# Eight attention rounds in another order on four engines, one Trainium2 core

## The reference

```python
x = L0(x)   # B=8, C=64, 16x16 pixels: N=256
            # q,k = Wq x + bq, Wk x + bk (8 channels); v = Wv x + bv (32 channels)
            # attn = softmax(q^T k); out = Wo (v attn^T) + bo; x = gamma*out + x
x = L1(x)   # the same with v of 64 channels and no Wo; x = x + out
x = L2(x)   # batch norm, relu, 3x3 conv with w = mean|w0| * sign(w0); again with w1; + x
x = L3(x)   # whitening by a Cholesky factor over 4 groups of channels, a 4x4 mix, bias
```

## Time and profile before

| | |
|---|---|
| median of 3 runs | 75.25 us (75.05 to 75.28) |
| profiled execution | 74.86 us, span 73.1 us |
| PE, PEld | 61.4 us (84%), 34.8 us (48%) |
| DVE, ACT, POOL | 50.4 us (69%), 46.6 us (64%), 26.9 us (37%) |
| mean of one DVE instruction | L877 684 ns, L901 684 ns, L887 482 ns, L907 422 ns, L917 484 ns |
| ACT, L458 | 446 ns, with 204 ns of reading the sum beside the next |
| fillers (L583) | six from 0.76 us on took 2.72 us, twelve from 42.90 us on 3.00 us |

### The profile page before, as it was taken

The page is one execution under the profiler, slowest core; times in us unless marked ns, Lnnn a source line. Parts: engine busy times, 40 slices in busy tenths (PEclk is TensorE's granted clock), DMA queues, the critical chain, the costliest instruction groups (busy, mean ns, idle before and its releaser), DMA issues.

```text
span 73.1 us, 1583 instructions
## 1 busy us (share of the span) xinstructions
PE 61.4 (84%) x512; PEld 34.8 (48%) x516; DVE 50.4 (69%) x134; ACT 46.6 (64%) x135; POOL 26.9 (37%) x68
## 2 busy tenths in 40 slices
PE   5968677489998999896939999799999889999910
PEld 2224534154553646444415573586745676774400
DVE  0067998587979888776993656899578994367340
ACT  1603589679898989899987527950069493535440
POOL 7005128702748475723050624460054600006300
PEclk9999999999999999999999999999999999999996
DMA  0888820000000000000000000000000000000025
GB/s 6 244 255 234 306 96 0 0 0 0 0 0 9 4 0 0 0 9 0 0 0 9 0 0 0 0 0 9 0 0 0 0 0 0 9 0 0 0 83 204
DMA packets 2167, 2.70 MB, mean 37 GB/s; under 512 B 368, under 2 KB 1520, under 8 KB 2160
## 3 DMA queue, kind: packets, MB, share of 16 engines
q1 hardware_dynamic: 1872, 2.41, 10.2%
q10 hardware_dynamic: 288, 0.20, 0.8%
HBM read 2.08 MB, written 0.52 MB: 36 GB/s over the span
## 4 chain that ended last, share of the span: by engine, by line
PE 49%; DVE 16%; ACT 13%; POOL 8%; issue 8%; POOLq 0%; ACTq 0%; DVEq 0%
PE bank L583 9%; PE bank L683 8%; ACT bank L458 7%; PE bank L739 5%; PE bank L593 4%; PE bank L617 4%; DVE cut L887 3%; PE bank L664 3%; PE bank L728 3%; DVE conv_in L991 3%; DVE conv_in L997 3%; ACT conv_in L511 2%; PE bank L764 2%; PE bank L772 2%; PE bank L649 2%
## 5 line engine op out<-in xcount | busy, mean ns | idle before, releaser
L458 ACT ACTIVATE bank<-bank,negmax 128x256 f32<-128x256 f32 x32 | 14.3, 446 | 1.2 <-DVE negmax L877 1.0
L583 PE MATMUL bank<-const-bfloat16-1.0 128*128 128x512 bf16 x52 | 14.1, 409 | 1.0 <-PEq L1164 0.8
L877 DVE TENSOR_REDUCE negmax<-bank 128x2 f32<-128x512 f32 x16 | 10.4, 684 | 1.4 <-PE bank L633 1.3
L739 PE MATMUL bank<-conv_in,taps 128*64 128x256 f16 x144 | 9.8, 279 | 1.0 <-DVE conv_in L997 0.7
L583 PEld LDWEIGHTS bank<-const-bfloat16-1.0 128*128 128x128 bf16 x56 | 5.6, 107 | 7.2 <-issue 2.5
L471 ACT ACTIVATE probs<-bank 128x512 f32<-128x512 f32 x16 | 8.6, 588 | 0.6 <-PE bank L654 0.5
L739 PEld LDWEIGHTS bank<-conv_in,taps 128*64 128x64 bf16 x144 | 7.3, 109 | 3.4 <-DVE conv_in L997 2.0
L683 PE MATMUL bank<-probs,vt 128*64 128x256 f32 x64 | 8.7, 391 | 0.0
L887 DVE TENSOR_SCALAR cut<-bank,prm 128x256 f32<-128x256 f32 x8 | 3.9, 482 | 5.8 <-PE bank L593 5.7
L511 ACT ACTIVATE conv_in<-z,bn_t,rstd 64x256 f16<-64x256 f32 x4 | 2.4, 601 | 6.8 <-POOL rstd L400 6.7
L458 ACT ACTIVATION_READ_ACCUMULATOR bank<-bank,negmax 128x1 f32 x32 | 6.5, 204 | 0.0
(11 more groups left out here) (130 smaller groups left out, 105.9 us busy)
## 6 DMA issues: line engine op xcount, KB each, us to landing
cw<-conv_w SPq DMA_DIRECT2D x2, 288.0 KB, 4.6
x<-x_in SPq DMA_DIRECT2D x4, 128.0 KB, 2.9
out<-res SPq DMA_DIRECT2D x2, 256.0 KB, 2.1
kst<-consts SPq DMA_DIRECT2D x1, 452.0 KB, 5.5
aw<-attn_w ACTq DMA_DIRECT2D x1, 128.0 KB, 2.5
aw<-attn_w SPq DMA_DIRECT2D x1, 128.0 KB, 3.6
half<-select SPq DMA_DIRECT2D x1, 96.0 KB, 2.9
kst<-consts SPq DMA_DIRECT2D x1, 64.5 KB, 3.9
```

Source lines behind the costliest of these rows:

```text
L458: nc.scalar.activation(part, part, ACT.Exp, bias=negmax[:, i % 2, n:n + 1], accum_out=total[:, i % 2, n:n + 1]).then_inc(total_out, 1)
L583: mm(bank[:], filler, filled, start=True, stop=True)
L739: last = mm(img(pb_conv[n][q][lanes(g), 0:N]), taps[n][:, k, :], conv_in[n][g][:, q, dy:dy + H, dx:dx + W], start=(k == 0), stop=(k == TAP ...
L877: ve.tensor_reduce(negmax[:, i % 2, g * CH:(g + 1) * CH], pb_s[(2 * i + g) % 3][:].rearrange("p (t n) -> p t n", t=CH), AX.X, ALU.max, neg ...
```

## The change

Of a round, the order on PE, ACT, DVE and POOL is written anew. `totals` becomes `sum_exps(i, g, t)` and `logs(i)`, `scores_t` loses its second half to `add_shifts(i)`, `exps(i, g)` and `mix(i, g)` take one image g of the pair at a time. On ACT the copy of the rows stands between the third and the fourth sum of the next round, and the logarithm behind the exps. On DVE `values_out(i + 1)` stands behind the maxima. On POOL all four memsets come first, `later_parts(2)` goes ahead of `shifts(0)`, and each `shifts(i)` waits for `later_parts(i + 2)`. One slice of x is issued by ACT in place of SP. The sums of |w| move from the end of the attention into rounds 4 to 6.

```diff
-WARM_START = (6, 1, 2)
-WARM_ATTENTION = (1, 1, 4, 2)
+WARM_START = (6, 1, 2, 2)
...
-        pb_mean = banks[7]
+        pb_mean = banks[4]
...
             sp.dma_start(prm[:], params).then_inc(prm_in, 16)
-            sp.dma_start(xs[0][:, quarter(1)], x[:, quarter(1)]).then_inc(x_in[1], 16)
             sp.dma_start(half[:], select).then_inc(half_in, 16)
...
-            nc.gpsimd.memset(zeroed[0], 0).then_inc(pads_set, 1)
+            for some in zeroed:
+                nc.gpsimd.memset(some, 0).then_inc(pads_set, 1)
...
-                pool.wait_ge(part2_out, 2 if i == 0 else min(max(i + 2, PAIRS), ITERS))
+                pool.wait_ge(part2_out, min(i + 3, ITERS))
...
             act.dma_start(aw[:, A_P0:A_V0], attn_w[:, A_P0:A_V0]).then_inc(p0_in, 16)
+            act.dma_start(xs[0][:, quarter(1)], x[:, quarter(1)]).then_inc(x_in[1], 16)
             act.dma_start(aw[:, A_V0:A_P1], attn_w[:, A_V0:A_P1]).then_inc(vo0_in, 16)
...
+            for g in range(G):
+                for t in range(CH):
+                    sum_exps(0, g, t)
+            logs(0)
+            for i in range(ITERS):
                 if i + 1 < ITERS:
-                    totals(i + 1, 0)
-                    totals(i + 1, 1)
-                exps(i)
+                    sum_exps(i + 1, 0, 0)
+                    sum_exps(i + 1, 0, 1)
+                    sum_exps(i + 1, 1, 0)
+                shift_rows(i)
                 if i + 1 < ITERS:
-                    shift_rows(i + 1)
+                    sum_exps(i + 1, 1, 1)
+                if i == ITERS - 2:
+                    logs(ITERS - 1)
+                exps(i, 0)
+                exps(i, 1)
+                if i < ITERS - 2:
+                    logs(i + 1)
...
+            def add_shifts(i):
+
                 pe.wait_ge(rows_out, i + 1)
...
+            def weight_means():
+
+                pe.wait_ge(kst_in, 16)
+                pe.wait_ge(wabs_out, 2)
+                pe.wait_ge(total_out, 2 * CH * (ITERS - 1))
...
             project(0)
             project(1)
             keep_warm(WARM_START[1], pb_t[0])
+            project(2)
             replicate(0)
             value_weights()
+            keep_warm(WARM_START[2], pb_t[0])
             scores(0)
-            project(2)
             replicate(1)
+            project(3)
             values(0)
+            keep_warm(WARM_START[3], pb_t[0])
             scores(1)
...
             for i in range(ITERS):
+                scores_t(i)
+                if i + 2 < ITERS:
+                    replicate(i + 2)
+                if i < ITERS - 1:
+                    shifts_to_rows(i)
                 if PAIRS <= i + 3 < ITERS:
                     project(i + 3)
+                add_shifts(i)
                 if i + 2 < ITERS:
                     scores(i + 2)
-                else:
-                    keep_warm(WARM_ATTENTION[i + 2 - ITERS], pb_rep)
                 if i + 1 < ITERS:
-                    shifts_to_rows(i + 1)
+                    values(i + 1)
                 if i == ITERS - 2:
-                    scores_t(ITERS - 1)
-                mix(i)
-                if i + 2 < ITERS:
-                    values(i + 2)
-                if i + 3 < ITERS:
-                    replicate(i + 3)
-                if i + 1 < ITERS - 1:
-                    scores_t(i + 1)
+                    weight_means()
+                mix(i, 0)
+                if i == ITERS - 2:
+                    shifts_to_rows(ITERS - 1)
+                mix(i, 1)
...
+                if i + 1 < ITERS:
+                    values_out(i + 1)
+                if 4 <= i < 6:
+                    weight_sum(i - 4)
+                if i == 6:
+                    power_of_two(1)
                 if i >= PAIRS + 1:
                     statistics(i - PAIRS - 1)
```

More of the change, by code:

```diff
@@ L365, in shifts @@
                                         ALU.subtract).then_inc(shift_out, 1)
-            pool.wait_ge(pads_set, 1)
+            pool.wait_ge(pads_set, len(zeroed))
             later_parts(1)
+            later_parts(2)
             shifts(0)
             pool.wait_ge(shift_out, 1)
-            later_parts(2)
             later_parts(3)
[L373 to L376, removed]
+            for i in range(1, ITERS):
+                shifts(i)
+                pool.wait_ge(shift_out, i + 1)
+                if i + 3 < ITERS:
                     later_parts(i + 3)
[L378 to L386, removed]
+                if i == 5:
+                    pool.wait_ge(prm_in, 16)
+                    pool.wait_ge(x_out, PAIRS)
+                    nc.gpsimd.tensor_scalar(base[:], x_of(ITERS - 1), prm[:, P_BV1:P_BV1 + 1], 1.0,
+                                            ALU.add, ALU.mult).then_inc(base_out, 1)
+                    pool.wait_ge(base_out, 1)
             pool.wait_ge(id_in, 16)
@@ L454, in totals, with logs, exps @@
                 act.wait_ge(max_out, 2 * i + g + 1)
[L455 to L465, removed]
+                n = g * CH + t
+                part = pb_s[(2 * i + g) % 3][:, t * N:(t + 1) * N]
+                nc.scalar.activation(part, part, ACT.Exp,
+                                     bias=negmax[:, i % 2, n:n + 1],
+                                     accum_out=total[:, i % 2, n:n + 1]).then_inc(total_out, 1)
+            def logs(i):
+                act.wait_ge(total_out, 2 * CH * (i + 1))
+                nc.scalar.activation(lntot[:, i % 2, :], total[:, i % 2, :], ACT.Ln).then_inc(ln_out, 1)
+            def exps(i, g):
                 if i >= 2:
                     act.wait_ge(pv_mm, i - 1)
[L469 to L472, removed]
+                act.wait_ge(t_mm, 2 * i + g + 1)
+                nc.scalar.activation(probs[:, i % 2, g], pb_t[g][:].rearrange("p (t n) -> p t n", t=CH),
+                                     ACT.Exp).then_inc(exp_out, 1)
             def shift_rows(i):
@@ L665, in shifts_to_rows, with mix @@
                 last.then_inc(rows_mm, 1)
[L667 to L674, removed]
-                else:
[L676 to L686, removed]
+            def mix(i, g):
+                if g == 0:
+                    pe.wait_ge(v_out, i + 1)
+                    if i < ITERS - 1:
+                        pe.wait_ge(part0_out, min(max(i + 4, PAIRS), ITERS))
+                        if i >= 1:
+                            pe.wait_ge(x_out, i)
+                    else:
+                        pe.wait_ge(rows_out, ITERS)
+                        pe.wait_ge(base_out, 1)
+                        pe.wait_ge(id_in, 16)
+                        mm(mixed(i), ident, base[:], start=True, stop=False, skip_group_check=True)
+                pe.wait_ge(exp_out, 2 * i + g + 1)
+                for t in range(CH):
+                    last = mm(mixed(i)[g * C:(g + 1) * C], vt[:, i % 2, t, g * C:(g + 1) * C],
+                              probs[:, i % 2, g, t, :], start=(t == 0 and i < ITERS - 1), stop=(t == CH - 1),
+                              skip_group_check=(i == ITERS - 1))
+                if g == 1:
+                    last.then_inc(pv_mm, 1)
@@ L688, in _ @@
+            def weight_means():
+                pe.wait_ge(kst_in, 16)
+                pe.wait_ge(wabs_out, 2)
+                pe.wait_ge(total_out, 2 * CH * (ITERS - 1))
+                for n in range(2):
+                    last = mm(pb_mean[:, n:n + 1], kst[:, K_ONES:K_ONES + P], wabs[n][:],
+                              start=True, stop=True)
+                last.then_inc(e_mm, 1)
             keep_warm(WARM_START[0], pb_t[0])
@@ L775, in gram @@
                     last.then_inc(gram_mm, 1)
[L777 to L782, removed]
             pe.wait_ge(x_out, ITERS - 1)
@@ L934, in _ @@
             queries_keys(0)
+            first_parts(2)
             maxima(0, 0)
@@ L937, in _ @@
             queries_keys(1)
-            first_parts(2)
+            first_parts(3)
             maxima(1, 0)
+            maxima(1, 1)
             values_out(0)
[L941 to L944, removed]
             for i in range(ITERS):
@@ L947, in _ @@
                     add_shortcut(i - 1)
-                if i + 1 < ITERS:
-                    values_out(i + 1)
-                if i >= 1 and i + 2 < ITERS:
+                if i + 2 < ITERS:
                     queries_keys(i + 2)
+                if i == 0:
+                    power_of_two(0)
                 if PAIRS <= i + 3 < ITERS:
```

22 lines of the change are left out of this document (2 added, 20 removed).

## The result

The changed kernel measured 76.13 us in the median against 75.25, and 1.0099 times the kernel before (95% interval 1.0051 to 1.0148): 1% slower, clear of its interval, where 74.0 was forecast.

A forecast was written before the change was run, and what follows sets the result against it. TensorE's chain was taken to bound middle rounds at 3.69 us, with waits at the start and a serial seam behind round 7. `rstd` at 42.33 for 43.61 saves 1.28: 75.25 - 1.28 = 74.0 us, range 73.2 to 74.9.

The forecast's parts named there:

- A round: Middle rounds: a chain through DVE's cut and POOL's parts takes 3.83 us, 0.14 more than TensorE's 3.69.
- three loops of a round: Middle rounds: POOL's parts 3.83 us, TensorE's own work 3.69, ACT's loop 3.45; the longest sets the round.
- The start: Before the rounds: slice on ACT and reordered queues bring `mix(0)` from 15.12 to 13.83; the start gains 1.0 us.
- rival (a): Start: late slice, or fillers and `project(2)`, hold up `replicate(0)`; up to 0.45 us later, 74.3 to 74.5; chance 0.12.
- The rounds: Middle rounds: 3.83 us each against 3.81 before, so they give nothing and cost nothing; rows(5) at 30.83.
- Rival (b): Middle rounds: five handovers in the parts' loop make 4.08 us for 3.83; kernel 74.8 to 75.0; chance 0.13.
- The end: Last rounds to `rstd`: `mv` at 41.56 against 43.15, `rstd` at 42.33 against 43.61, leaving a gain of 1.28 us.
- the cover: Before `rstd`: POOL's idle 1.29 us is used up; `rstd` waits for `taps` until 42.28, giving back 0.3.
- Rival (d), the clock: Start: TensorE idle some 1.3 us lets its clock fall, adding 1.5 to 3.0 us: 75.5 to 77; chance 0.08.
- three signs of being wrong: In the changed profile: rows(1) to rows(5) over 16 us, `mix(0)` later than 14.5, or a slice with lower granted clock.

The follow-up runs named there:

- The seventh mix whole: The changed kernel with the last rows moved from between the seventh mix's halves to behind both: 75.24 to 77.23 us, no ratio.

## Why the prediction was wrong

**The step that failed is "A round": the price and the place of `mix`.** I took its 1.02 as 0.51 for each image, one behind the other, so that the second image's exps, 0.5 later, were in time. The 1.02 are two halves side by side on TensorE, 1.0 each. With the exps 0.48 apart and the mix at their heels, the second half starts late, and the mix takes 1.45. Of my three loops of a round (POOL's parts 3.83, TensorE's work 3.69, ACT 3.45) none went through the mix; but a round now needs its exps before its mix and its mix before the next rows. By the timeline of the changed kernel: rows at 21.36, `add_shifts` at 22.11 (0.75), exps at 22.59 (0.48), the first matmul behind the second exps at 23.73 (1.14), end of the mix at 24.81 (1.08), next rows at 25.31 (0.50): 3.95, and the loop closes. Before, the next round's rows stood ahead of a round's mix:

```profile
22.52 0.29 PE L664 MATMUL bank<-half,shift 128*128 128x128 f16 x2 [0.26 <-POOL shift L364]
...
25.32 1.08 ACT L471 ACTIVATE probs<-bank 128x512 f32<-128x512 f32 x2
...
26.48 1.09 PE L683 MATMUL bank<-probs,vt 128*64 128x256 f32 x8
```

Both exps had ended (26.40) when the mix began, so its halves ran side by side. And from a round's rows to its mix it was 3.96 there too, but the next rows (26.27) did not wait for that mix; the path had two rounds to close in, and this loop of one round did not exist.

The Trainium skill (TensorE: Matmul & The Clock Gate, "Part 3: Packing small matmuls — row/col tiling") says that matmuls on different tiles of the array run concurrently. The trace agrees: eight passes in 1.02 together, four in 1.0 alone; eight took 1.45 where the second half came 0.4 late. I had not applied it, though the rows of the order said it: each matmul of `mix` is 64x256, so its weights fill 64 columns (128*64 in the timeline), where those of a projection fill 128.

Point by point, at full clock (the changed kernel with its pause filled), against the forecast:

| | forecast | measured | difference so far |
|---|---|---|---|
| `mix(0)` | 13.83 | 14.17 | +0.34 |
| rows(1) | 15.42 | 16.12 | +0.70 |
| rows(5) | 30.83 | 31.85 | +1.02 |
| rows(7) | 37.56 | 38.63 | +1.07 |
| exps(7) | 38.87 | 40.56 | +1.69 |
| `mv` | 41.56 | 44.02 | +2.46 |
| `rstd` | 42.33 | 44.48 | +2.15 |

Of the 2.15 some 1.9 lie in the mixes and in the rounds that they set.

- **The start** was right in mechanism: the rows wait for `values_out(0)`, and `mix(0)` came 0.9 earlier than before. Of the 0.34 the larger part is rival (a): the third slice landed 3.59 after issue, at 5.68, and `project(2)` held up `replicate(0)`. In the profiled execution of "The seventh mix whole" it landed at 5.13 and `mix(0)` came at 13.94, with the first cut as late (4.57) as here (4.65). It is worth nothing without the new rounds, though: there `mix(0)` has to stand behind rows(1), and those did not move. That POOL held `mix(0)` was right, but it was not the only path: the one over `scores(2)` ended at almost the same time.
- **The rounds**: +0.36 in the first mix, +0.32 in the four rounds of 3.93 on average. Rival (b) had the direction (it said 4.08 for 3.83, against 3.93 measured), with the wrong cause: POOL's loop didn't bind, ahead of the rows nothing waited. And that nobody waited for POOL in the rounds of before was a misreading: three of the five transpositions from rows(2) to rows(6) waited for it, 0.24 to 0.26 each.
- **The end**: +0.62 from splitting the seventh mix (the two halves 2.2 for 1.44, of which 0.3 can be won back), and +0.77 from exps(7) to `mv`, of which 0.6 is the last mix: its end lies 2.2 behind the start of the exps, where I had 1.62 (38.87 to 40.49), because here too the halves start apart (1.56). DVE's weight sum delayed nothing that counted: scores(7) stood behind `add_shifts`, which waited for the copy of the rows.
- **`taps`**: the cover was not used up. `mv` came so late that POOL was idle 0.53 ahead of `rstd`; the 0.3 that I had given back there were not due.
- **Rival (d), the clock**, happened, beside the loss and not as its cause: it adds about 1.2 to `mix(0)` (15.36 for 14.17), in a part of the executions. Of my three signs of being wrong two came with it, a lower clock and `mix(0)` later than 14.5; rows(1) to rows(5) took 15.7, not over 16. I gave it 0.08, taking the pause as 1.3 (it was 1.08), with the argument that pauses of 0.9 had left the clock full in one profile. One profile can't say that: the same stretch is disturbed in other executions of the kernel before.

## What to carry to other kernels

Before a reordering, ask of each short step whether its time is that of one piece or of several side by side, and what each half alone would take: separating them, by a wait or by an instruction between, can double it while the chain of waits shows nothing but a busy engine. Draw the loop through every step that is moved next to its producer, not only through the engines that look busy. And where a kernel is as short as this, look at TensorE's pauses one by one: five fillers took the changed kernel's spread from 2.7 us (75.7 to 78.4, on one chip) to 0.5 (on two others, with 12 executions each, at most 0.6), and those added to the kernel before cost nothing.

## What the hardware showed unexpectedly

- Two halves of a product on different columns of TensorE overlap only as far as they are ready together and stand side by side in the queue: 1.02 us for eight passes together, 1.45 with the second half 0.4 late, 2 x 1.0 with another instruction between.
- A pause of 1.08 us of TensorE (11.41 to 12.48) was followed by 0.57 of the clock from 13 to 17 us; filled with five matmuls, 24 of 24 executions had a mean clock of 0.990 or more. The same pause stood in one profile at full clock, so it does not bring the fall every time.
- In some executions TensorE works at the slow pitch until 12 us (1.22 a projection for 0.70), while the page's granted clock reads 1.00 for that stretch. The clock row shows falls, not a late rise: durations have to be looked at too, or where the trace's first record of the clock begins (12.79 us there). Of four kernels run side by side, the three with a gap between the first two projections (slice on SP) had 8, 5 and 4 of 12 executions over 76.7, the one without (slice on ACT, seventh mix whole) none, and the kernel before had 21 of 35 over 76.3. That the gap decides fits these, and is not shown: the filling of the gap by itself was tried beside a kernel before that hardly had outliers.
- Moving one transfer of 128 KB from SP to ACT made the others land later (3.5 for 2.9), and none of the issue time saved arrived. Over all profiles the third slice, issued 0.47 earlier, landed at 5.59 to 6.14 us in eight of nine with the slice on ACT (5.13 in the ninth), and at 5.15 to 5.49 in the seven with it on SP. The Trainium skill (DMA: Bandwidth & Descriptors, "Issuing engines are not separate DMA queues") allows only the issue time as a gain; here it was less than that.
